# An attention and mixture-of-experts kernel: later blocks' statistics, turns and queries leave the head, and passes alternate with turned key pieces

## What is computed

```
x = x + tanh(g_xattn) * attention(layernorm(x), ctx, Wq, bq, Wk, bk, Wv, bv)
x = x + tanh(g_ffn)   * experts(layernorm(x), W1, b1, W2, b2, Wr, br)

attention: query = xn @ Wq + bq;  key = ctx @ Wk + bk;  value = ctx @ Wv + bv
           softmax(query @ key.T / sqrt(128)) @ value
experts:   top 2 of softmax(xn @ Wr + br), renormalised; relu(xn @ W1[e] + b1[e]) @ W2[e] + b2[e]
```

## Time and profile before

| | before |
|---|---|
| median of 3 runs | 282.98 us (282.55 to 285.04) |
| the profiled execution's own time | 281.82 us |
| its span | 280.1 us |
| mean granted clock of TensorE | 0.991 of full |
| PE busy | 268.3 us (96%) |
| DVE busy | 210.6 us (75%) |
| ACT busy | 186.6 us (67%) |
| POOL busy | 109.6 us (39%) |

### The profile page before, as it was taken

One profiled execution on the slowest core, in us unless ns is written; L12 is line 12 of the kernel. 1 busy time (PEld: TensorE's weight loads), 2 busy tenths in 40 slices (PEclk: granted clock), 3 DMA queues, 4 the chain that ended last, 5 costly groups with the idle time before them and its releaser, 6 DMA issues.

```text
span 280.1 us, 5068 instructions
## 1 busy us (share of the span) xinstructions
PE 268.3 (96%) x1662; PEld 246.6 (88%) x1662; DVE 210.6 (75%) x406; ACT 186.6 (67%) x338; POOL 109.6 (39%) x144
## 2 busy tenths in 40 slices
PE   7899999999999999999999999989999999994994
PEld 6678999999999999999899999978989989993994
DVE  4889977995686997898456688667797895643796
ACT  3996565446566556556579888797457557965891
POOL 3899993556600030000006346710153434375130
PEclk9999999999999999999999999999999999999898
DMA  6700020000199000000000342443011112141112
GB/s 199 255 2 0 4 76 0 2 1 2 42 292 276 1 2 0 0 4 1 0 2 4 84 140 63 148 148 103 19 32 28 30 30 67 49 114 28 60 47 84
DMA packets 18485, 17.08 MB, mean 61 GB/s; under 512 B 2410, under 2 KB 14940, under 8 KB 18460
## 3 DMA queue, kind: packets, MB, share of 16 engines
q1 hardware_dynamic: 17372, 15.31, 18.0%
q0 software_dynamic: 640, 1.31, 1.6%
q10 hardware_dynamic: 448, 0.14, 0.2%
HBM read 13.34 MB, written 3.42 MB: 60 GB/s over the span
## 4 chain that ended last, share of the span: by engine, by line
PE 84%; DVE 8%; issue 4%; DMA 2%; ACT 1%; SPq 1%; DVEq 0%; another core or an unknown queue 0%; ACTq 0%
PE ps L1448 8%; PE ps L1474 8%; PE ps L1449 8%; PE ps L1476 8%; PE ps L1475 8%; PE ps L1450 7%; PE ps L1370 7%; PE ps L1575 4%; PE ps L1561 3%; PE ps L1602 2%; DVE pmax L975 2%; PE ps L1641 2%; PE ps L1600 2%; PE ps L1643 2%; PE ps L1642 2%
## 5 line engine op out<-in xcount | busy, mean ns | idle before, releaser
L882 ACT ACTIVATE ex_hi<-ps 128x768 fp32r<-128x768 f32 (+1 forms) x78 | 56.9, 730 | 57.7 <-PE ps L1450 54.4
L1190 DVE TENSOR_TENSOR ex_lo<-ps,ex_hi 128x768 fp32r<-128x768 f32 (+1 forms) x66 | 58.5, 886 | 24.5 <-ACT ps L886 18.8
L975 DVE TENSOR_REDUCE pmax<-ps 128x1 f32<-128x512 f32 (+2 forms) x74 | 62.4, 875 | 10.2 <-PE ps L1370 9.5
L1474 PE MATMUL ps<-ex_hi,ctx_both 128*97 128x384 f32 (+1 forms) x153 | 49.8, 325 | 0.0
L886 ACT ACTIVATE ps<-ps 128x768 f32<-128x768 f32 (+1 forms) x66 | 49.7, 752 | 0.0
L1449 PE MATMUL ps<-q_lo,ctxT_hi 96*128 96x384 f32 (+1 forms) x153 | 49.1, 321 | 0.0
L1450 PE MATMUL ps<-q_hi,ctxT_lo 96*128 96x384 f32 (+1 forms) x153 | 48.7, 318 | 0.0
L1476 PE MATMUL ps<-ex_lo,ctx_both 128*97 128x384 f32 (+1 forms) x153 | 48.6, 318 | 0.0
L1475 PE MATMUL ps<-ex_hi,ctx_both 128*96 128x384 f32 (+1 forms) x153 | 48.6, 318 | 0.0
L1448 PE MATMUL ps<-q_hi,ctxT_hi 97*128 97x384 f32 (+1 forms) x126 | 42.6, 338 | 1.5 <-DVE ex_lo L1190 1.4
L1370 PE MATMUL ps<-ctxT_hi,q_hi 97*128 97x512 f32 (+1 forms) x104 | 34.3, 400 | 0.6 <-DVE pmax L975 0.4
(11 more groups left out here) (227 smaller groups left out, 547.3 us busy)
## 6 DMA issues: line engine op xcount, KB each, us to landing
raw<-in_ctx_dram SPq DMA_DIRECT2D x6, 384.0 KB, 6.4
w_raw<-in_L_ffn_W_dram SPq DMA_DIRECT2D x8, 256.0 KB, 3.9
raw<-in_L_ffn_W_dram SPq DMA_DIRECT2D x8, 256.0 KB, 6.3
raw<-in_L_ffn_b_dram SPq DMA_DIRECT2D x8, 256.0 KB
shared<-routing SPq DMA_DIRECT2D x8, 192.0 KB
x_slots<-shared SPq DMA_DIRECT2D x1, 1088.0 KB, 6.3
y_slots<-shared SPq DMA_DIRECT2D x17, 64.0 KB, 1.5
shared<-in_L_ffn_b_dram SPq DMA_DIRECT2D x1, 512.0 KB, 3.8
```

Source lines behind the costliest of these rows:

```text
L882: nc.scalar.activation(ex_pair(ex_hi, u % P_RING, js, n), scores, ACT.Exp)
L975: nc.vector.tensor_reduce(pmax[:, FIRST_TILE[ROUND_BLOCK[r]] + t, place:place + 1], max_home(s)[:, 0:w], AX.X, ALU.max).then_inc(max_reduc ...
L1190: nc.vector.tensor_tensor(ex_pair(ex_lo, u % P_RING, js, n), whole, ex_pair(ex_hi, u % P_RING, js, n).bitcast(F32), ALU.subtract).then_inc ...
L1474: nc.tensor.matmul(dst[0:CA, :], ch[:, j, :], hi, start=(j == first), stop=False)
```

## The change

Four things change, all in the head and in block 0. The diff is cut to its core.

- The six filler transposes after the fold (WARM_NORM) are gone.
- In the head, PE no longer turns windows 2 and 3 ahead of the first pass and later windows in pairs. It turns two windows, makes the query, and then one window follows each of the six passes (windows 2 to 7).
- Block 1's and block 2's statistics go to DVE's units 3 and 10, their turns to units 6 and 15, their queries to units 8 and 17, their q_lo to units 9 and 18. On POOL, block 1's inverse deviation and normalised tokens stand behind ctxT_lo of windows 4 to 6, block 2's behind the last split of the keys.
- Unit 10 loses its pass, unit 14 gets a second one.

```diff
-    FIRST_BLOCK_PASSES = [0, 1, 1, 0, 1, 1, 1, 1, 1, 1, 1, 0, 1, 1, 1, 2, 2, 2, 2, 2, 2, 2, 2, 1, 0, 0]
+    FIRST_BLOCK_PASSES = [0, 1, 1, 0, 1, 1, 1, 1, 1, 1, 0, 0, 1, 1, 2, 2, 2, 2, 2, 2, 2, 2, 2, 1, 0, 0]
...
-        QK_UNIT = {1: 1, 2: 8}
-        TURN_X_UNIT = {2: 6}
-        SPLIT_UNIT = {1: 2, 2: 9}
+        QK_UNIT = {1: 8, 2: 17}
+        TURN_X_UNIT = {1: 6, 2: 15}
+        STATISTICS_UNIT = {1: 3, 2: 10}
+        SPLIT_UNIT = {1: 9, 2: 18}
...
             pool.wait_ge(ones_ready, 1)
-            inverse_deviation(1)
-            normalize(1)
...
                 split_ctxT(w)
             for g in range(0, 2):
                 split_ctx(g)
-            inverse_deviation(2)
-            normalize(2)
             for w in range(4, 7):
                 split_ctxT(w)
+            inverse_deviation(1)
+            normalize(1)
             split_ctx(2)
             for w in range(7, TURNED_BY_VECTOR):
                 split_ctxT(w)
             for g in range(3, NG):
                 split_ctx(g)
+            inverse_deviation(2)
+            normalize(2)
...
             copy_ctxT_whole(TURNED_BY_VECTOR - 1)
-            copy_x(1)
...
             last.then_inc(first_norm, 1)
-            dve.wait_ge(x_later_in, 16)
-            statistics(0, 1)
-            statistics(0, 2)
             split_q(0)
...
+                    for later, unit in STATISTICS_UNIT.items():
+                        if b == 0 and i == unit:
+                            dve.wait_ge(x_later_in, 16)
+                            statistics(0, later)
...
-            keep_warm(WARM_NORM, MPAIR[:, 0, :])
...
             make_qk(0)
-            for w in range(2, 4):
-                turn_window(w)
             for s in range(SLOTS_UNTIL[0]):
                 score_for_max(s)
-                w = 4 + s
-                if s % 2 and w < TURNED_BY_VECTOR:
-                    turn_window(w - 1)
-                    turn_window(w)
-            turn_window(TURNED_BY_VECTOR - 1)
-            pe.wait_ge(ctxT_f_ready, TURNED_BY_VECTOR - 3)
-            turn_x(0, 1, x_home(1))
-            for w in range(TURNED_BY_VECTOR, NW - 2):
+                turn_window(s + 2)
+            for w in range(SLOTS_UNTIL[0] + 2, NW - 2):
                 turn_window(w)
             turn_max(0)
...
                 if u < 2:
                     pe.wait_ge(ctxT_f_ready, TURNED_BY_VECTOR)
-                    pe.wait_ge(x_copied, 2)
```

More of the change, by code:

```diff
@@ L47 @@
 WARM_FOLD = 4
-WARM_NORM = 6
 EPS = 1e-5
@@ L417, in x_home @@
         def x_home(b):
-            return [UB[0], ps[:, TURNED_BY_VECTOR % 4, :], UB[1]][b]
+            return UB[1] if b else UB[0]
         def flat(pair):
@@ L1379, in turn_max @@
                 if r == 1:
-                    pe.wait_ge(q_lo_ready, NB)
+                    pe.wait_ge(q_lo_ready, 2)
                 for t in range(BLOCK_TILES[b]):
@@ L1411, in beside_first_block @@
                         pe.wait_ge(q_lo_ready, b)
+                        if unit > ROWS_UNIT:
+                            pe.wait_ge(rows_copied, 1)
                         turn_x(0, b, x_home(b))
```

## The result

The changed kernel takes 292.62 us in the median (291.83 to 293.64, 4 runs), the kernel before 282.77 beside it: a ratio of 1.033, 95% interval 1.027 to 1.039. It is slower, as forecast, but by 9.9 us and not by 4.1: outside the range. The profiled execution took 293.64 us (span 291.9, mean granted clock 0.971), 11.8 more than the one before.

What follows compares the result with a forecast made beforehand. PE was taken to bound the kernel (84% of the chain), with ACT and DVE nearly full in the head. The terms summed to +4.1 us, 281.82 to 285.9, or 287.1 us on the median's footing; range 283.8 to 289.4.

Steps and rivals of the forecast that it cites:

- term 1: Head: ACT's copies wait for PE's turns, gaps 1.95 us less block 1's xT 0.49, so +1.45 us.
- Term 5: Unit 12 of block 0: PE waits for the second round's row behind block 2's statistics, +0.8 us, bounds 0 and 1.2.
- So I keep full speed: Head and block 0: granted clock stays 1.00 despite PE's gaps, so no time is added for the clock.
- rival D: Head: the clock falls to 1.2 GHz, up to 6 us more, 293 us; chance 0.04.
- 2: Head, unit 1's query: removing its two matmuls only lengthens PE's wait for ex_lo, so 0 us.
- 3: Unit 3: block 1's statistics on DVE delay unit 4's reduction, partly covered, +0.25 us, bounds 0 and 0.75.
- 4: Unit 6, block 1's turn: PE waits for POOL's norm, +0.85 us, and the turn's own work adds +0.25.
- 6: Unit 8: block 1's query now stands in a full PE stretch, +0.36 us, bounds 0.3 to 0.6.
- term 7: Unit 18: block 2's q_lo on DVE makes the next passes wait some, +0.15 us, bounds 0 and 0.5.
- 8: Head: removing six filler transposes changes nothing, the time going into a DMA wait, 0 us, bounds 0 and -0.3.
- B: Only the head and PE's added work count, later waits find cover: +2.2 us, 285.2 us; chance 0.15.
- C: Head: reductions, not ACT, end it, so the kernel is not slower, 282.9 us; chance 0.13.

Runs made afterwards that it cites:

- both experiments that removed the hold: Changed kernel with block 2's rstd and norm before POOL's last two context subtractions, ratio 1.019; changed kernel with block 2's epsilon addition moved to POOL, 288.31 us, ratio 1.022.
- the first trace: Profiled execution of the changed kernel in its first measurement: 293.64 us; median 292.62 us, ratio 1.033 to the kernel before.
- the second: Changed kernel run again with no edit: 291.67 us, ratio 1.034 to the kernel before.
- the wait filled: Changed kernel with twenty filler transposes on PE ahead of unit 12's row wait, run on two chips: ratios 1.022 and 1.020 to the kernel before.
- the experiment in which POOL waits: Changed kernel with block 2's rstd and norm before POOL's last two context subtractions instead of behind them: ratio 1.019 to the kernel before.
- the first pair: Traces of the kernel before and the changed kernel from the first measurement: medians 282.77 and 292.62 us, ratio 1.033.
- the filled pair: Fillers ahead of three waits in the changed kernel (unit 12, block 2's unit 21, experts), of the last two in the kernel before: 289.98 and 282.70 us.

## Why the prediction was wrong

The sign was right, and so was what the forecast said of the head and of unit 6. Where nothing held DVE the distance at block 1 came out too: +4.0 in both experiments that removed the hold, for a forecast of +4.1. In part that is luck: in the first of them the first exponential came 0.74 later where term 1 had 1.45, and the terms behind it came out larger, 3.27 for 2.66. Two steps failed.

**Term 5, the row at unit 12: 0.8 forecast, 2.14 measured.** Its sum took the statistics at the 1.2 us that they cost in the head, and its upper bound was "the whole statistics". In the head POOL had no two-input subtraction beside them; at unit 10 it splits the keys one group after another. With the hold removed the wait is 0.68 and 0.48. The missed 1.4 to 1.5 is a price of the new neighbourhood, not of the instructions moved.

**"So I keep full speed": wrong in block 0.** The section on the clock asked only whether the head would fall below its share of work, and rival D put the fall there. It fell behind the one long wait instead: 3.0 us lost in the first trace, 1.5 in the second (34.04 and 32.58 from unit 12 to block 1, for 31.06 with the wait filled). That D's 293 lies near the 292.6 measured is chance: the head kept its time. Waits near the forecast's 0.8 did not lower it (0.68 and 0.48), so this loss hangs on the first mistake. The earlier trace rows had shown the pattern: 0.81 at 255 to 260, where PE was idle for more than half. I read it as a remark on the tail and gave a wait no price beyond its length.

The sum that the runs show up to block 1 is then 1.2 in the head, 3.3 from the first exponential on without the hold (the experiment in which POOL waits), 1.5 for the hold and 3.0 for the clock: 8.9 us, as in the first trace. The 2.9 behind it stand with waits and clock falls that both kernels have. In the first pair the changed kernel drew 2.11 us at 193.94 with a fall to 0.50 behind it, the kernel before 1.25 at 184.19 without one; the filled pair has no such loss up to the end of block 2. For the 0.6 that the experts added, and for 1.3 and 3.6 in the other two pairs of traces, that is not shown.

The other terms: 1, +1.45 forecast, +1.39 from q_hi on and +1.2 with q_hi's own start; the reading that the copies followed "without a gap" missed the 0.45 us of the kernel before. 2, nothing, as forecast: unit 2's scores come 1.96 us behind the first exponential in both kernels. But the 0.56 of the earlier trace rows is idle time of the weight loads, put down to issue; PE's own wait for ex_lo was 0.17 and grew to 0.81. 3, +0.25: unit 6's scores went from 29.48 to 30.87, 0.2 beyond the head's share. 4, 0.85 of waiting, 0.76 measured. 6 and 7, with the pass that comes back and block 2's turn: 1.34 forecast between unit 12 and block 1, 1.7 measured (31.06 less 29.37). PE has no gap of 0.05 us or more there; the query and the turn cost what was forecast, and the distances from the passes' matmuls to the next add up to 9.50 us (experiment in which POOL waits) instead of 8.46, for one pass more at 0.58. So term 7 was near 0.5 and not 0.15. 8, nothing in the total, but for a reason that I had read from a blind column. Of the rivals, B falls with the waits at units 6 and 12, C with the first exponential, E was not seen: POOL was in time for unit 15.

## What to carry to other kernels

A moved instruction brings its own duration and takes on what its new neighbours do to it: before work goes beside another engine's, look for instructions of both engines that use the same ports (by the rule cited above), and bound the moved one by the neighbour's whole length. A wait of the tensor engine is not always paid at its own length: look at the granted clock behind the longest waits of the trace, and price a new wait of that length with the slow stretch as well, here 1.5 or 3.0 us on top of 2.14. Put the operand that the critical engine waits for ahead of everything that can be late without harm, here the row ahead of the statistics: one unit's shift gave back 5.5 of 8.9 us.

## What the runs showed of the hardware

- A tensor_scalar of DVE on 3 numbers per partition, SBUF to SBUF: 0.17 us alone; beside a 1.7 us two-input subtraction of POOL 1.61 to 1.67 where it came at the subtraction's start (six traces), 1.17 and 0.23 where it came later. It ended within 0.03 us of the subtraction each time. bn_stats, the aggregate and an addition with an operand in PSUM were not held.
- PE waits and the granted clock behind them: after single waits of 0.48 to 1.29 us it stayed at 1.00. Of the eleven between 1.96 and 2.16 us, eight were followed by 0.50 and three (1.97, 2.01, 2.09) were not; one of 1.74 was, 1.53 and 1.69 were not; behind each from 2.24 to 3.66 us it was at 0.50. These rows set no limit. It was low for 3.4 or for 6.8 us. In block 0, with PE full, that cost 1.5 and 3.0.
- The clock column reads 1.00 over the first microseconds even where PE is slow; the matmuls' own lengths (421 ns for 272, up to 10.1 us in one trace) tell.
- A filler transpose costs 117 ns at full clock, and 137 to 170 where the clock was low for part of it (4.10 and 5.10 us for thirty).
- On one chip ACT, DVE and PE stand still for 1.3 to 3.7 us near 180 and 255 us without a missing operand that the trace shows; on another they do not. It is worth 7.3 us or more in 280, more than the forecast change. Its cause is open.
